# Layer 1 attention: the scores of two heads under one exponential, the maxima one head at a time

## The reference, cut to what matters

```python
q = rmsnorm(apply_rope((h @ Wq + bq).reshape(batch, seq, 16, 8)), qn_w)
k = rmsnorm(apply_rope((h @ Wk + bk).reshape(batch, seq, 4, 8)), kn_w)
v = (h @ Wv + bv).reshape(batch, seq, 4, 8)
k = jnp.repeat(k, 4, axis=2)
v = jnp.repeat(v, 4, axis=2)
scores = jnp.einsum('bthd,bshd->bhts', q, k) / np.sqrt(8)
causal = jnp.tril(jnp.ones((seq, seq), dtype=bool))
scores = jnp.where(causal[None, None], scores, -jnp.inf)
attn = jax.nn.softmax(scores, axis=-1)
out = jnp.einsum('bhts,bshd->bthd', attn, v)
```

## Time and profile before

| | |
|---|---|
| median of 3 runs | 1730.03 us (1722.28 to 1730.83) |
| the profiled execution, its own time | 1734.56 us |
| its span in the profile | 1732.8 us |
| PE busy over the span | 1441.4 us (83%) |
| DVE busy | 1129.3 us (65%) |
| ACT busy | 692.5 us (40%) |
| mean granted TensorE clock | 0.884 of full |

### The profile page before, as it was taken

How to read it: one execution, slowest core, us unless ns; L and a number is a source line. 1 busy time by engine, 2 the same in 40 slices (tenths; PEclk the granted TensorE clock), 3 DMA queues, 4 the chain that set the end, 5 groups by cost and what they waited for, 6 DMA issues and landing times. The chain is left out here.

```text
span 1732.8 us, 20831 instructions
## 1 busy us (share of the span) xinstructions
PE 1441.4 (83%) x6716; PEld 852.5 (49%) x6716; DVE 1129.3 (65%) x1721; ACT 692.5 (40%) x1256; POOL 170.4 (10%) x205
## 2 busy tenths in 40 slices
PE   3889999999999999429999996731699999748996
PEld 3345555554545554226666664531344444225785
DVE  4645646464646552368999998573767776146997
ACT  1133333323232333025555553421156665524663
POOL 0000100001010100001111110021011211101110
PEclk9689999999999999759999997865589998767998
DMA  2000110101010101104444441005112220112220
GB/s 72 5 9 6 25 28 7 33 0 33 0 33 0 33 4 25 28 13 105 108 108 108 108 110 38 1 1 159 36 27 57 67 57 17 30 27 84 95 91 25
DMA packets 41517, 78.47 MB, mean 45 GB/s; under 512 B 18880, under 2 KB 31048, under 8 KB 36808
## 3 DMA queue, kind: packets, MB, share of 16 engines
q1 hardware_dynamic: 40304, 69.03, 15.1%
q0 software_dynamic: 1152, 8.65, 2.4%
HBM read 69.20 MB, written 7.93 MB: 45 GB/s over the span
## 5 line engine op out<-in xcount | busy, mean ns | idle before, releaser
L582 ACT ACTIVATE shared<-ps 128x1024 f32<-128x1024 f32 (+7 forms) x256 | 165.8, 650 | 408.5 <-PE ps L428 252.1
L1216 PE MATMUL ps<-qA 128*96 128x512 f32 (+1 forms) x1152 | 305.1, 401 | 13.1 <-DVE qA L1328 10.4
L444 PE MATMUL ps<-shared,Vg 128*65 128x512 f32 (+3 forms) x768 | 295.5, 494 | 7.5 <-ACT shared L582 4.3
L495 DVE TENSOR_REDUCE mraw<-ps 128x1 f32<-128x512 f32 (+3 forms) x304 | 196.9, 660 | 112.0 <-PE ps L395 83.7
L1216 PEld LDWEIGHTS ps<-qA 128*96 128x96 f32 (+1 forms) x1152 | 192.3, 172 | 98.4 <-DVE shared L1341 21.1
L900 DVE TENSOR_REDUCE mraw<-ps 128x2 f32<-128x1024 f32 (+3 forms) x160 | 175.0, 1116 | 92.2 <-PE ps L820 68.8
L944 ACT ACTIVATE shared<-ps 128x512 f32<-128x512 f32 (+2 forms) x320 | 154.5, 562 | 138.6 <-PE ps L836 138.4
L391 PE MATMUL ps<-kH,qA 128*128 128x512 f32 (+3 forms) x384 | 185.2, 512 | 17.0 <-DVE mraw L495 13.2
L426 PE MATMUL ps<-qA,kH 128*128 128x512 f32 (+3 forms) x384 | 191.0, 498 | 2.7 <-DMA qB<-mT 2.7
L1270 ACT CAST qA<-shared 96x512 fp32r<-96x512 f32 (+1 forms) x192 | 119.2, 621 | 163.1 <-DVE shared L1348 162.5
L1227 PE MATMUL ps<-qA,kH 96*128 96x512 f32 (+1 forms) x576 | 165.4, 396 | 4.0 <-DVE qA L1322 4.0
(11 more groups left out here) (254 smaller groups left out, 1695.0 us busy)
## 6 DMA issues: line engine op xcount, KB each, us to landing
shared<-comb SPq DMA_DIRECT2D x32, 768.0 KB, 5.1
rB<-a0rec_dram POOLq DMA_DIRECT2D x8, 1024.0 KB, 7.0
shared<-comb SPq DMA_DIRECT2D x8, 1024.0 KB, 4.5
q_split<-qA SPq DMA_DIRECT2D x8, 512.0 KB
qA<-q_split SPq DMA_DIRECT2D x16, 256.0 KB, 4.4
rB<-a1rec_dram SPq DMA_DIRECT2D x32, 128.0 KB, 2.7
e0wUp<-in_w SPq DMA_DIRECT2D x64, 48.0 KB, 4.4
wqk<-in_wqk SPq DMA_DIRECT2D x8, 192.0 KB, 2.4
```

Source lines behind the costliest of these rows:

```text
L444: ins = nc.tensor.matmul(O[0:65, lo:hi], k.Vg[par][:, kt, :], k.PT[:, slot % PTR, lo:hi], start=(kt == 0), stop=(kt == 4 * ch + 3))
L495: ins = nc.vector.tensor_reduce(out, bank[:, 0:n_h * width].rearrange("p (h w) -> p h w", w=width), AX, ALU.max)
L582: nc.scalar.activation(k.PT[:, slot % PTR, kt * P:S], score_banks(slot)[:, kt * P:S], ACT.Exp, scale=scale).then_inc(p_full, 1)
L1216: ins = nc.tensor.matmul(bank[0:M, :], w[par][:, at:at + M], h[:, cols], start=(r == 0), stop=(r == 2))
```

## The change

Banks 0 and 1 hold the scores of two heads (i = 0 and 1 in two neighbouring banks), banks 2 and 3 those of the other two; ACT takes both banks with one exponential of 1024 elements per partition. A light unit has one such job with all four heads. The ring is two such pairs. That leaves banks 4, 5 and 6 for the maxima: a max job is now one i (one 64-row half) in one bank, 40 per group instead of 20, in a ring of three, and a max on the diagonal gets its mask before the other half's matmul follows. The list of due jobs is spread by the same formula over 42 entries instead of 22.

```diff
-    SCORE_BANKS = 3
+    MAX_BANKS = 3
...
         if 512 - unit_lo(n) > 256:
-            return [(h % 2, (h,)) for h in range(REP)]
-        return [(i, (i, i + 2)) for i in range(2)]
+            return [(0,), (2,)]
+        return [(0, 2)]
...
-                out += [(qt, ch, (0, 1))] if w <= 256 else [(qt, ch, (j,)) for j in range(2)]
+                out += [(qt, ch, i, js) for js in ([(0, 1)] if w <= 256 else [(0,), (1,)]) for i in range(2)]
...
-        def pair_banks(x):
-
-            return k.ps[:, (3 + 2 * (x % 2)) * 512:(5 + 2 * (x % 2)) * 512].rearrange("p (i n) -> p i n", i=2)
-
-        def score_bank(s):
-            return k.bank(s % SCORE_BANKS)
+        def max_bank(x):
+
+            return k.bank(4 + x % MAX_BANKS)
+
+        def score_banks(s):
+            return k.ps[:, 2 * (s % 2) * 512:2 * (s % 2 + 1) * 512].rearrange("p (i n) -> p i n", i=2)
...
-                    if idx >= 2:
-                        pe.wait_ge(x_free, idx - 1)
+                    if idx >= MAX_BANKS:
+                        pe.wait_ge(x_free, idx - MAX_BANKS + 1)
...
-                        for i in range(2):
-                            rows = row_tile(i, 64)
-                            ins = nc.tensor.matmul(pair[:, i, slot * w:(slot + 1) * w],
+                        ins = nc.tensor.matmul(bank[:, slot * w:(slot + 1) * w],
...
                     if diagonal:
                         for slot in range(len(js)):
-                            for i in range(2):
-                                ins = nc.tensor.matmul(pair[:, i, (slot + 1) * w - P:(slot + 1) * w], k.ident_bf[:, :],
-                                                       k.masks[:, 1, :], start=False, stop=True,
-                                                       skip_group_check=True)
+                            ins = nc.tensor.matmul(bank[:, (slot + 1) * w - P:(slot + 1) * w], k.ident_bf[:, :],
+                                                   k.masks[:, 1, :], start=False, stop=True, skip_group_check=True)
...
-                    if s >= SCORE_BANKS:
-                        pe.wait_ge(p_done, s - SCORE_BANKS + 1)
+                    if s >= 2:
+                        pe.wait_ge(p_done, s - 1)
...
-                        if at % 2 == 1 or not jobs:
-                            share = -(-len(fills) // max(len(jobs) // 2 - at // 2, 1))
-                            for idx in fills[:share]:
-                                max_job(idx)
-                            fills = fills[share:]
+                        share = -(-len(fills) // (2 * max(len(jobs) - at, 1))) * 2
+                        for idx in fills[:share]:
+                            max_job(idx)
+                        fills = fills[share:]
...
-                    src = pair[:, :, 0:len(js) * w].rearrange("p i (j w) -> p i j w", w=w)
-                    nc.vector.tensor_reduce(out[:, :, js[0]:js[-1] + 1, qt % 4], src, AX, ALU.max).then_inc(x_free, 1)
+                    src = bank[:, 0:len(js) * w].rearrange("p (j w) -> p j w", w=w)
+                    nc.vector.tensor_reduce(out[:, i, js[0]:js[-1] + 1, qt % 4], src, AX, ALU.max).then_inc(x_free, 1)
...
-                            dst = probs(n)[:, hs[0]:hs[-1] + 1:2, lo:512]
-                            src = score_bank(s)[:, 0:len(hs) * (512 - lo)].rearrange("p (a q) -> p a q", a=len(hs))
+                            dst = probs(n)[:, hs[0]:hs[-1] + 2, lo:512]
+                            src = score_banks(s)[:, :, 0:512 - lo]
+                            if len(hs) == 2:
+                                dst = dst.rearrange("p (a i) q -> p i a q", i=2)
+                                src = score_banks(s)[:, :, 0:2 * (512 - lo)].rearrange("p i (a q) -> p i a q", a=2)
                             nc.scalar.activation(dst, src, ACT.Exp, scale=scale).then_inc(p_done, 1)
```

More of the change, by code:

```diff
@@ L795, in max_job @@
                     kind, qc, n = GROUP_JOBS[j]
-                    pair = pair_banks(idx)
-                    if idx >= 2:
-                        pe.wait_ge(x_free, idx - 1)
+                    bank = max_bank(idx)
+                    if idx >= MAX_BANKS:
+                        pe.wait_ge(x_free, idx - MAX_BANKS + 1)
                     if kind == "turn":
                         pe.wait_ge(folded, 2 * g + qc + 1)
-                        nc.tensor.transpose(pair[0:16, 0, 0:P], k.mmax[:, 16 * qc:16 * qc + 16],
+                        nc.tensor.transpose(bank[0:16, 0:P], k.mmax[:, 16 * qc:16 * qc + 16],
                                             k.ident[:, :]).then_inc(x_full, 1)
@@ L805, in max_job, with score_job @@
                         pe.wait_ge(in_ld[g % 3], 16 * LOADS * (g // 3 + 1))
[L806 removed]
+                    qt, ch, i, js = MAXES[qc][n]
                     w = keys_in(qt, ch)
                     diagonal = ch * 512 + w == (qt + 1) * P
+                    rows = row_tile(i, 64)
                     for slot, jj in enumerate(js):
[L810 to L816 removed]
+                        ins = nc.tensor.matmul(bank[:, slot * w:(slot + 1) * w],
+                                               Q[g % 3][rows, jj, qt * P:(qt + 1) * P],
+                                               kZero[g % 3][rows, ch * 512:ch * 512 + w],
+                                               start=(slot == 0), stop=not diagonal, skip_group_check=True)
                     if diagonal:
                         for slot in range(len(js)):
[L819 to L822 removed]
+                            ins = nc.tensor.matmul(bank[:, (slot + 1) * w - P:(slot + 1) * w], k.ident_bf[:, :],
+                                                   k.masks[:, 1, :], start=False, stop=True, skip_group_check=True)
                     ins.then_inc(x_full, 1)
[L825 removed]
+                def score_job(n, s, hs):
                     g, (qc, kt) = n // NU, UNITS[n % NU]
@@ L829, in score_job @@
                         pe.wait_ge(m_row[qc], 64 * (g + 1))
-                    if s >= SCORE_BANKS:
-                        pe.wait_ge(p_done, s - SCORE_BANKS + 1)
+                    if s >= 2:
+                        pe.wait_ge(p_done, s - 1)
                     lo = unit_lo(n)
                     w = 512 - lo
-                    rows = row_tile(i, 64)
                     for slot, h in enumerate(hs):
[L836 to L839, removed]
+                        for i in range(2):
+                            rows = row_tile(i, 64)
+                            ins = nc.tensor.matmul(score_banks(s)[:, i, slot * w:(slot + 1) * w],
+                                                   kOne[g % 3][rows, kt * P:(kt + 1) * P],
+                                                   Q[g % 3][rows, h // 2, qc * 512 + lo:(qc + 1) * 512],
+                                                   start=True, stop=True)
                     ins.then_inc(s_full, 1)
@@ L864, in _ @@
                         if at < len(jobs):
[L865 to L870 removed]
+                            score_job(n, first_score[n] + at, jobs[at])
+                        share = -(-len(fills) // (2 * max(len(jobs) - at, 1))) * 2
+                        for idx in fills[:share]:
+                            max_job(idx)
+                        fills = fills[share:]
                     if n >= LAG:
@@ L891, in take @@
                             dve.wait_ge(m_row[qc], 64 * g)
-                        nc.vector.tensor_scalar(k.mT[0:16, qc, :], pair[0:16, 0, 0:P], -1.0, None, ALU.mult)\
+                        nc.vector.tensor_scalar(k.mT[0:16, qc, :], bank[0:16, 0:P], -1.0, None, ALU.mult)\
                             .then_inc(x_free, 1)
```

4 lines of the change are left out of this document (2 added, 2 removed).

## The result

The changed kernel takes 1794.47 us as the median of four runs (1769.68 to 1806.22) against 1728.3 us before (now four runs), which is a ratio of the medians of 1.038. Two of the four runs lie over 1.5% above the fastest and count as slow; the fast ones alone give 1.031, 95% interval 1.019 to 1.043. The forecast was 1734 us, no change, within 1708 to 1762. The runs of the changed kernel also spread four times as far as those before, 36.5 us against 8.6, and go by the mean granted clock, 0.880 in the fastest and 0.856 in the slowest.

A forecast was written before the change was run, and what follows sets the result against it. PE was taken as the bound, with PE and ACT waiting for each other. Steady groups +5, start +4 and +4, last group -7, turns -1.5 gave +4.5 us: 1734 or 1735 on the runs' scale, no change, range 1708 to 1762.

The forecast's parts named there:

- The maxima one half at a time: Diagonal max pairs: matmul and mask of each half in turn, +0.4 us per pair, +4.8 per group (+2.5 to +6.6).
- The ring of scores: Score pairs wait for an exponential a whole unit earlier; PE's wait for ACT nearly goes, -4.4 us per group (1.6 to 5.4).
- the late fourth score: A unit's fourth score matmul waiting for an exponential; removal taken as worth 0.55 us per full unit (0.2 to 0.67).
- rival 4: Slower: two heads wait for the later one, so the ring frees late as before; chance 0.25 together with rival 1.
- Rival 1: Slower: halves in turn decide, late fourth score worth only 0.2 us per unit; +24 us, 1754; chance 0.25 with rival 4.
- The ring of three maxima: Max jobs have three banks, so PE runs only three heads ahead; with split pairs +0.5 us per group.
- split pairs: Off-diagonal max pairs with values between their halves lose 0.23 us, at most eight times a group; within the +0.5 us.
- The clock: Granted clock of the middle groups, with no term for a fall in the sum; a fall stood only in rival 3.
- rival 3: Slower: one more group's clock falls to 0.66, +9 us, or two groups +18, 1752; chance 0.08.
- The last group: Eight full units whose fourth score loses 0.94 us, nearly all won: -7 us, between -4 and -8.
- The start: Halves in turn ahead of the first unit, +4 us, and in the first units, +4 (0 to +9).
- the turns: Transposes after the maxima, shorter where right behind a max, ten of 16 against six: -1.5 us over all.

The follow-up runs named there:

- experiment 1: Kernel before, with one edit: in diagonal max jobs the first half's mask comes before the second half's matmul; 1795.24 us, ratio 1.041.
- experiment 7: Changed kernel with max matmuls on all 128 rows, each adding up the scores of both heads of the pair; 1751.69 us, ratio 1.014.
- experiment 5: Kernel before with all max jobs of a full unit placed between its third and fourth score; 1740.05 us, ratio 1.006.
- experiment 6: Experiment 2 with DVE reducing only the first half of each block of keys; 1719.91 us, ratio 0.995.
- experiment 2: Changed kernel with both halves' max matmuls ahead of both masks, issued in pairs that wait for both banks; 1753.61 us, ratio 1.017.
- experiment 9: Kernel before with the wide exponential and its two-pair ring only from the last group's third unit on; 1723.0 us, ratio 0.9954.
- experiment 11: Experiment 1 with max matmuls on all 128 rows, each adding up the scores of both heads of the pair; 1760.99 us, ratio 1.018.
- experiment 3: Changed kernel with each mask added by two 64-row matmuls on its own head's half; 1749.52 us, ratio 1.013.

## Why the prediction was wrong, by its own steps

**The maxima one half at a time: right in kind, a little high in size.** I put +4.8 us per group; experiment 1 shows +3.3 and +3.7 at full clock. The pair of 384 columns takes 0.95 us where I reckoned 0.9 to 1.0. The gaps had the size that I said; my reason for the one ahead of the mask was wrong, as experiment 7 shows. The Trainium skill's rule (TensorEngine Tiling (Array Packing), Tiling Modes: a change of mode drains the engine) agrees with the 0.15 against 0.04 us behind the mask. It does not explain the 0.33 ahead of the mask, which experiment 7 has without a change of mode.

**The ring of scores: a term of the sum that failed.** I priced the late fourth score at 0.55 us per full unit, 4.4 per group, from two timelines in which it was late. Removing it gave 0.4 us per group (experiment 5) or 1 (experiment 6, with DVE out of the way). I had added up a wait without asking what the unit would do next without it. Nor did the wait nearly vanish, as I had said it would: it fell from 67.4 to 35.5 us over the stage (which also speaks against rival 4, that the wide exponential frees nothing). Rival 1 had this step right in kind, and its 0.2 us per unit was still too much. What exactly sets the 29 us that then remain, with PE's records at 26 to 27, DVE at 16 and ACT at 19, stays open.

**The ring of three maxima: the term was mis-sized.** I put +0.5 us per group for it and for split pairs. With the order repaired (experiment 2) PE waited 19.3 us for DVE in 62 us, and halving the reduces took a group from 31 to 29: about 2 us. In the changed kernel itself these waits were only 26 us over the stage, 9 more than before, because its PE was slower and each half waited for its own bank alone; there the term stayed near its forecast.

**The clock: put at nothing in the sum, and the step that failed most.** It stood only in rival 3, with a chance of 0.08, priced at +9 us per group with a low clock, for two groups. It came in five of the six middle groups, at +7 us in experiment 1's group of 0.75, and it was about half of the loss. The price was off too: 28 us of PE at a mean clock of 0.66 instead of 1.00 become 28 / 0.66 = 42, so +14 where PE sets the pace (an estimate), and not a third more. I argued from four groups that had held 1.00 "with many such gaps already". But those gaps had both halves at work in between; maxima by lone halves were new, and I had no row for them.

**The last group: right in kind, and larger.** -7 forecast, within -4 to -8, and -10.3 measured; the clock rose with it from 0.66 to 1.00, which I had not counted on and which is the likely rest. The start was forecast at +8 and came to +12, which one profile can't tell from +8; the turns can't be told apart.

With what experiments 1, 6 and 9 measured the sum reads: order 3.4 x 6 = 20, start 12, last group -10, three banks less what the ring gives, about +1 x 6 = 6, together 28; the stage lost 57. The other 29 us are the clock in the six middle groups, an estimate by subtraction. The windows allow it: by their clocks these groups ran at half clock for about 109 us, against 18 before, and 91 us more of it cost at most half of that, 46. That the three banks' share is taken from experiment 2, where it was larger, makes the 29 rather too small.

## What to carry to other kernels

When two matmuls share the array by halves, look at the order of everything else that is issued between them: one full-width instruction in between costs the overlap, and it can cost the clock too, which was worth more here. A wait seen in a timeline is an upper bound for what its removal gives; move the waiting instruction first, which costs no banks, and see. And use a resource-hungry form where the resource is idle: here the last group, where the wide exponential took 10 us off and nothing had to be paid for it. Count what an idea needs at the start of the kernel as well: the masks on 64 rows cost about 5 us there, more than the 0.6 us at most that they gave in groups 3 and 4.

## What the runs showed of the hardware that I had not expected

The granted clock went with the use of both halves of the array. Middle groups with maxima by lone halves ran at 0.68 to 0.91 (the changed kernel) and at 0.75 to 0.95, but also twice at 1.00 (experiment 1); the same order on 128 rows, with more work for PE, ran at 1.00 in eight of twelve groups (experiments 7 and 11). PE's busy share was no guide: 43.3 of 45.3 us at a clock of 0.71 in the changed kernel, 27.0 of 31.5 us at 1.00 in experiment 2. Lone halves are not the whole of it, for the start of experiment 2 ran at 0.61 without lone maxima. What decides in a single group whether the clock falls stays open.

An fp32 matmul of 512 columns and a bf16 mask into the same bank start 0.32 to 0.34 us apart whether the matmul uses 64 or 128 rows, when the mask uses 128: about 0.1 us more than the stream of 0.23. With a mask on the same 64 rows (experiment 3) the 0.1 us was gone where nothing ran beside: 0.18 us behind a matmul of 384 columns, instead of 0.27.
